# Fixed pads in front of the expert regions, a second silu for the rounded form, and router products placed among other products

## The reference

```python
x = x + 0.5 * moe(layernorm(x))      # first expert phase
x = x + attn(layernorm(x))           # attention block
x = x + 0.5 * moe(layernorm(x))      # second expert phase, the same weights

def moe(x):                          # 8 experts, hidden size 512, top 2
    logits = silu(x @ rw1 + rb1) @ rw2 + rb2
    w = softmax over the two largest logits, 0 elsewhere
    h = silu(x @ we1[e] + be1[e])
    return x + sum_e w[e] * (h @ we2[e] + be2[e])

def attn(x):                         # 16 heads of 64
    x = x + linear_attention(LN1(x)) # phi = elu + 1, causal: cumulative
                                     # sums of K V and K; num / den; @ Wo
    return x + gelu(LN2(x) @ Wf1) @ Wf2
```

## Time and profile before

| what | value |
|---|---|
| runs | 1998.72, 2001.55, 2002.62 us |
| profiled execution | 2005.34 us |
| its span | 2003.6 us |
| PE busy | 1698.4 us (85%) |
| DVE busy | 1558.9 us (78%) |
| ACT busy | 1072.6 us (54%) |
| POOL busy | 968.9 us (48%) |
| DMA, mean | 95 GB/s |

### The profile page before, as it was taken

How to read it: one execution, slowest core, us unless ns; L and a number is a source line. 1 busy time by engine, 2 the same in 40 slices (tenths; PEclk the granted TensorE clock), 3 DMA queues, 4 the chain that set the end, 5 groups by cost and what they waited for, 6 DMA issues and landing times. The chain is left out here.

```text
span 2003.6 us, 36381 instructions
## 1 busy us (share of the span) xinstructions
PE 1698.4 (85%) x12527; PEld 1384.7 (69%) x12527; DVE 1558.9 (78%) x4234; ACT 1072.6 (54%) x1935; POOL 968.9 (48%) x1010
## 2 busy tenths in 40 slices
PE   4448799984999999999999999999999956799990
PEld 3236688863778777777777777777777745687770
DVE  7667687765888888988888888898888626577774
ACT  2125577753556556555565555655556424577770
POOL 4876401115544465555546546445553324566661
PEclk9998899996999999999999999999999967899995
DMA  7554677740000010000001001001000004577757
GB/s 228 190 179 132 227 254 263 264 156 13 12 9 9 9 20 18 11 19 19 12 16 20 16 12 21 18 9 20 17 12 12 12 11 180 201 235 249 231 195 266
DMA packets 91664, 190.31 MB, mean 95 GB/s; under 512 B 15021, under 2 KB 52570, under 8 KB 80474
## 3 DMA queue, kind: packets, MB, share of 16 engines
q1 hardware_dynamic: 45738, 131.26, 19.3%
q0 software_dynamic: 33840, 46.17, 8.7%
q10 hardware_dynamic: 11904, 10.55, 1.5%
HBM read 131.08 MB, written 56.85 MB: 94 GB/s over the span
## 5 line engine op out<-in xcount | busy, mean ns | idle before, releaser
L1551 POOL TENSOR_TENSOR at_sc<-at_sc 128x512 f32<-128x512 f32 x128 | 198.2, 1548 | 344.4 <-DVE at_sc L1651 344.1
L551 ACT ACTIVATE f_hid<-f_up_ps,f_w 128x512 f32<-128x512 f32 x312 | 214.3, 688 | 155.0 <-PE f_up_ps L426 126.3
L1643 DVE SCALAR_TENSOR_TENSOR at_qk<-at_exps,at_relus 128x512 f32<-128x512 f32 x256 | 182.8, 715 | 100.5 <-ACT at_relus L1460 97.9
L1651 DVE TENSOR_TENSOR at_sc<-at_s_ps,mask 128x384 f32<-128x384 f32 x512 | 251.7, 550 | 1.1 <-PE at_s_ps L1284 1.1
L892 DVE TENSOR_TENSOR f_hid_lo<-f_hid,f_hid_hi 128x512 fp32r<-128x512 f32 x312 | 209.2, 688 | 14.8 <-ACT f_hid_hi L558 3.1
L665 POOL DMA_INDIRECT expert_rows<-f_rows_out,f_dest x156 | 165.3, 1059 | 97.1 <-DVE f_rows_out L915 60.5
L1958 POOL DMA_INDIRECT x<-finished_rows,slot x120 | 195.7, 1631 | 29.7 <-issue 29.7
L1524 ACT ACTIVATE raw<-at_num_ps 128x512 f32<-128x512 f32 x128 | 76.1, 595 | 241.2 <-PE at_num_ps L1321 220.6
L648 POOL DMA_INDIRECT sent_rows<-f_xn,slot x144 | 148.8, 1034 | 69.5 <-issue 40.8
L1281 PE MATMUL at_s_ps<-at_qk 64*128 64x256 f32 x1024 | 172.0, 413 | 6.7 <-issue 4.3
L1459 ACT ACTIVATE at_exps<-at_proj_ps 128x512 f32<-128x512 f32 x253 | 152.4, 603 | 36.2 <-PE at_proj_ps L1259 29.4
(11 more groups left out here) (324 smaller groups left out, 4802.8 us busy)
## 6 DMA issues: line engine op xcount, KB each, us to landing
f_w<-split_weights SPq DMA_DIRECT2D x78, 1028.0 KB
f_got<-sent_rows SPq DMA_DIRECT2D x78, 264.0 KB, 4.7
finished_rows<-f_rows_out POOLq DMA_DIRECT2D x39, 256.0 KB, 2.5
split_weights<-f_split SPq DMA_DIRECT2D x8, 1024.0 KB
sent_rows<-f_pads SPq DMA_DIRECT2D x16, 264.0 KB
x<-in_L_attn_x SPq DMA_DIRECT2D x16, 256.0 KB, 5.1
raw<-in_L_ffn_we SPq DMA_DIRECT2D x16, 256.0 KB
out_x<-x ACTq DMA_DIRECT2D x16, 256.0 KB, 4.4
```

Source lines behind the costliest of these rows:

```text
L551: A(hid[:, c, :], up_bank(n)[:, :], ACT.Silu, bias=w[:, i % RING_W, 4 * HID + c:4 * HID + c + 1].bitcast(FP32)).then_inc(s_silu, 1)
L1551: g.tensor_tensor(sc[:, n % RING_SC, :, 3, :], sc[:, n % RING_SC, :, 1, :], sc[:, n % RING_SC, :, 2, :], ALU.add).then_inc(s_sum, 1)
L1643: stt(full, exps[:, p % 2, :], 1.0, relus[:, p % 2, :], ALU.min, ALU.add).then_inc(s_phi, 1)
L1651: last = tt(flat(sc[:, (n // 2) % RING_SC, 2 * (n % 2) + half, 0:3, :]), s_ps[2 * (n % 2) + half][:, 0:3 * P], flat(mask[:, :, :]), ALU.mult)
```

## The change

It has four parts.

1. **Pads.** `region_starts` is now 512 + e·REGION: every region has 512 pad records in front, at a fixed place, and the tail region has moved with it. The last tile of an expert no longer starts at a multiple of 512 from the region's start but 512 rows ahead of the region's end, so it ends with the expert's last row; where an expert has fewer than 512 rows it begins in the pad. Rows that the tile before has computed already are computed again. So no pads are written behind the regions: `pad_end`, `s_ends` and f2's pad records on POOL are gone. The fills of the front pads are issued by ACT at f1's start, and the eight of the tail region on ACT's queue at the end of iteration t = 9, after DVE has changed the token numbers in the pad records. DVE works out the clipped starts in the table, in f1 the moves of places have three steps for each expert (24 in place of 16), and in f2 rows that a tile does a second time get a destination that nothing reads (`dest_twice`, and `row_of`, `unused`, `done_rows` made once).
2. **Silu.** The high part is a second silu from the same PSUM bank, rounded on output, right behind the first one. ACT's copy and DVE's cast are gone; `low` waits for one semaphore, `s_hi`, and so does `up`, since the bank is read twice.
3. **Order of the joint stage.** The four logit products of a token tile stand between the products of `down` and `up` of the tile's first expert part, the wait for `s_r1` stands ahead of that part; `router_hidden` of the next tile is ahead of the fourth expert part; ACT applies the router's silu at the end of the iteration before and the gate's tanh after the first expert part; DVE reads the places ahead of `route(t, 1)`, and makes `x_lo` ahead of `route(t, 2)`.
4. **Attention.** A logit product stands behind the denominators of unit 0 and of unit 1, and the counts behind those of unit 2; the bank isn't cleared by them (`start=False`).

The diff, cut to its core:

```diff
@@ fills and tables
             def fill(engine, r, i):
-            engine.dma_start(k.sent[bass.ds(r, TILE), :].rearrange("(p q) d -> p (q d)", q=TQ),
+            engine.dma_start(k.sent[r:r + TILE, :].rearrange("(p q) d -> p (q d)", q=TQ),
-            def pad_end(e):
-                fill(sp, sp.value_load(ends[0:1, e:e + 1], min_val=0, max_val=E * REGION - TILE), e)
...
-                if i == with_rows + 2:
-                    sp.wait_ge(s_pads, n_pads)
-                    sp.wait_ge(s_ends, 1)
-                    for e in range(E):
-                        pad_end(e)
             sp.wait_ge(s_table, 4)
...
-            sp.wait_ge(s_ended, 16 * (2 * E if loads else E))
+            if loads:
+                sp.wait_ge(s_ended, 16 * 2 * E)
             load_rows(EARLY)
...
+                if before:
+                    tt(passed_counts[:, :, :], passed[:, own, :], count_steps[:, :].unsqueeze(1).broadcast_to([P, n, E]),
+                       ALU.mult).then_inc(s_tab, 1)
...
+                    step(base + 8)
+                    v.tensor_reduce(tile_count[:, :], passed_counts[:, :, :], AXIS_X, ALU.add).then_inc(s_tab, 1)
+                    step(base + 9)
+                    stt(tile_row[:, own], tiles_before[:, own], -float(TILE), rest_rows[:, :], ALU.mult, ALU.add).then_inc(s_tab, 1)
+                    step(base + 11)
+                    stt(clipped[:, :], tile_count[:, :], counts[:, 0:1], tile_row[:, own], ALU.add, ALU.min).then_inc(s_tab, 1)
+                    step(base + 12)
+                    if out is not None:
+                        tt(done_rows[:, own], tile_row[:, own], clipped[:, :], ALU.subtract)
@@ ACT: fills of the start, and of the tail region
-                    fill(act, E * REGION + i * TILE, i)
+                    fill(act, i * REGION, i)
...
+                if loads and t == 1 + E:
+                    act.wait_ge(s_pads, 4)
+                    for n in range(E):
+                        fill(act, E * REGION + TILE + n * TILE, n)
@@ ACT: silu and high
             def high(n):
-                act.wait_ge(s_silu, n + 1)
                 if n >= HC:
                     act.wait_ge(s_down, n - HC + 1)
-                A(hid_hi[:, n % HC, :], hid[:, n % HC, :], ACT.Copy).then_inc(s_hi_odd if n % 2 else s_hi_even, 1)
+                A(hid_hi[:, c, :], up_bank(n)[:, :], ACT.Silu,
+                  bias=w[:, i % RING_W, 4 * HID + c:4 * HID + c + 1].bitcast(FP32)).then_inc(s_hi, 1)
...
                     silu(m // HC, m % HC)
-                if m < ALONE:
                     high(m)
-                elif m % 2 == 0 and m - 1 >= ALONE and m - 1 < HC * NTILES:
-                    high(m - 1)
@@ DVE
-                if m >= ALONE and m % 2 == 0 and m < HC * NTILES:
-                    high_even(m)
@@ PE: up and down with the logits between
                 mm(u[:, :], hi, eT_hi[:, b, :], start=True, stop=False)
+                if t is not None:
+                    logits(2)
                 mm(u[:, :], hi, eT_lo[:, b, :], start=False, stop=False)
+                if t is not None:
+                    logits(3).then_inc(s_logit, 1)
...
                 mm(o[:, :], hi, hid_hi[:, c, :], start=(c == 0), stop=False)
+                if t is not None:
+                    logits(0)
                 mm(o[:, :], hi, hid_lo[:, c, :], start=False, stop=False)
+                if t is not None:
+                    logits(1)
@@ DVE, f2: place_rows
+                    stt(dest_twice[:, :], row_of[:, :], done_rows[:, i:i + 1], unused[:, i, :], ALU.is_lt, ALU.mult)
+                    last = stt(dest_once[:, :], is_first[:, :], -float(TOKENS), row[:, :, TOKEN], ALU.mult, ALU.add)
+                elif step == 4:
+                    last = tt(dest[:, i % RING_DEST, :], dest_once[:, :], dest_twice[:, :], ALU.max)
@@ attention: denominators
                         last = mm(num_ps[32 * j:32 * j + 32, 0:BT], den_sel[:, u, :], sc[:, (UNITS * s + u) % RING_SC, j, 0:4:3, :],
                                  start=(u == 0), stop=(u == UNITS - 1))
+                    if u < BQ and r is not None:
+                        logits(u)
+                    if u == BQ and t is not None:
+                        count_places(t)
```

More of the change, by code:

```diff
@@ L63, in ffn_phase @@
     T = k.tiles
-    RING_OUT = 5 if out is None else 7
+    RING_OUT = 4 if out is None else 7
     assert 2 * TILE * begin - E * (TILE - 1) > (EARLY - 1) * TILE
@@ L483, in _ @@
                 else:
+                    pe.wait_ge(s_route, 7 * order(T - 1) + 1)
                     pe.wait_ge(s_pl, 3 * order(T - 2) + 1)
+                if t < T and i >= 0:
+                    expert_part(i, 0, t)
+                elif i >= 0:
+                    expert_part(i, 0)
+                elif t < T:
+                    for q in range(TQ):
+                        last = logits(q)
+                    last.then_inc(s_logit, 1)
                 if t > start and t in (begin, T):
@@ L774, in _ @@
                     dve.wait_ge(zeroed, k.n_zeroed)
-                v.tensor_copy(pads[:, :, :, TOKEN], k.spare[:, E:2 * E, :] if loads else k.spare[:, 0:E, :]).then_inc(s_pads, 1)
+                v.tensor_copy(pads[:, :, :, TOKEN], k.spare[:, 0:E, :]).then_inc(s_pads, 1)
                 if loads:
@@ L930, in expert_part @@
                         place_rows(i, 2)
-                        if PLACED == 4:
+                        if out is not None:
                             place_rows(i, 3)
                     if m == at + 2:
-                        place_rows(i, PLACED)
+                        for part in range(3 if out is None else 4, PLACED + 1):
+                            place_rows(i, part)
                 for i in range(NTILES):
```

190 lines of the change are left out of this document (98 added, 92 removed).

## The result

The changed kernel takes 2034.01 us in the median of four runs (2030.47 to 2035.20), the kernel before 2001.35 (1998.72 to 2002.62): ratio 1.0166, 95% interval 1.0148 to 1.0183. The changed kernel is slower by 33 us. The forecast was 1995, 6.5 us faster, with a range that ended at 2013.

The account below looks back on a forecast made before the run. PE was taken as the limit wherever nothing holds it up. Terms −11 − 5 + 1 + 16 − 5 − 3 = −7 took the profiled 2005.34 us to 1998.3, 1994.5 in the median, say 1995; range 1978 to 2013.

Parts of the forecast that it names:

- late row loads: Steady expert tiles, both phases: copy-out behind two silus on ACT delays SP's row loads; +16 us, bounds 0 and +36.
- Rival A: Steady expert tiles: row loads come the whole 0.58 us late, costing 36 us in place of 16; 2014.5 us, chance 0.15.
- central case: Whole kernel: all terms as estimated, about 1995 us, own range 1987 to 2003, chance 0.35.
- −3: Attention: logits' weight loads hidden beside denominators (at most −15) against array shape changes (+9); taken as −3 us.
- Rival B: Attention: changes of array shape drain TensorE, +9 us in place of a 3 us gain; 2006.5 us, chance 0.12.
- −11: Second phase's start: pads off SP's queue end PE's wait for rows; −11 us, bounds −16 and −7.
- Rival C: Idle stretches without releaser stay, only moved: second phase's pads −8, first phase's 0; 2002.5 us, chance 0.20.
- Pads in the first phase: End of first phase's routing: pad writes off SP recover part of 12.0 us lost; −5 us, bounds 0 and −10.
- the table's and the moves' extra steps: Longer table of tiles costs 1.2 us in each phase's pad term; DVE's extra moves of places cost nothing.
- the fills at +1: First phase's pure routing stage: eight pad writes on ACT's queue, mostly hidden; +1 us, bounds 0 and +5.
- The joint order's −5: Joint stage of routing and expert tiles: PE's wait for `f_places` shrinks; −5 us, bounds −14 and +5.

Follow-up runs that it names:

- second pair of traces: Changed kernel and kernel before, both unedited, run and traced again on one chip: 2038.03 us and 2011.42 us.
- second group: Follow-up runs on one chip where the kernel before took 2008.57 us; the unedited changed kernel took 2038.03 us there, ratio 1.0152.

## Why the prediction was wrong

**Silu twice: right mechanism, a second wait put at nothing.** The step was "late row loads", +16. Measured are +11.0 and +14.4 (+8.4 and +13.9 in the second pair of traces), 25 in all, and +18.7 for this part alone in a group without idle times. The forecast followed `s_outT` to SP's queue and did not ask who else waits for it. PE does, at the transposes back. In the first phase's stage 262 to 440 the wait for rows grew by 6.5 us (1.2 to 7.7), where the forecast had 6.4; the 5.7 for the copy-out, 17 times 0.33, came on top. (In the second phase both waits are there too, but the view puts a part of them down to "issue", so their shares are not read there.) So the term of the sum that failed is this one: slack of 0.29 at the transposes back against a copy-out later by 0.58. It could have been read from the kernel before, from the copy-out's end at 303.00 to the transposes back at 303.35; the view of waits could not show it, since nothing waited there yet. Rival A had the sign, and by row loads alone 36 us, 2014.5, with a chance of 0.15. Measured distances of tiles (6.89 and 7.08) lie between the central case's (6.7 and 6.9) and A's (7.0 and 7.2), so it had the size no better than the forecast, and not the mechanism.

**Attention: the sign was wrong.** −3 was taken "nearer to nothing than to either end"; it is +6.7 in the first comparison, +7.2 in the second group and +11.2 in the group without idle times. Rival B had +9 by 0.11 for each change of shape, and this is what happened: 0.12 for each, in steps with two to five changes more. That the stage with idle times shows only 7 of it has no cause shown. The hope that the logits' weight load hides beside wide denominators failed: a pair takes 0.32 among them and 0.27 ahead of them, and the denominators themselves go slower in pieces. The rule of the Trainium skill ("TensorEngine Tiling (Array Packing)", Key Properties) that a change of mode drains TensorE agrees with these traces, at 0.12 us a change. I had weighed it and set it below my own estimate, though the one row that I had pointed the same way.

**Pads, second phase: the wait went and another took its room.** −11 was 8.9 for the wait and its low clock, 3.7 as a share of ACT's idle time, less 1.2. The wait went from 6.93 to 1.33. But POOL's run of indirect DMAs had more to do, since the rows of two tiles were ready for it when the sendings ended, not of one: 24 issues without a break in 32 us, where the kernel before had 20 in 27, and ACT stood idle twice beside them. The step that failed is the room: the forecast took it that PE would go on as soon as no pads held the row load, and credited 0.6 of ACT's idle time to the pads as well. Rival C said that idle times without a releaser stay, and gave −8 for them; they stayed, and in this pair they grew (6.64 and 4.47 became 9.40 and 4.37; 5.86 and 4.50 became 12.20 in the second pair). That they grew because POOL's run did is argued, not shown. I had the evidence in the joint stage: `f_lg` on DVE starting 1.4 after POOL's last sending. I used it for that stage only. Without idle times there was no wait to win: the pads alone changed nothing (1.0012).

**What held.** Pads in the first phase, in sign: −5 forecast, −4.7 measured, but −13.7 in the second pair of traces, where the kernel before had lost more, so that −4.7 fits so well is luck. Then the table's and the moves' extra steps (nothing to be seen), the fills at +1 against +2.5 with the joint order in it. The joint order's −5 came to −0.7, within its bounds; its own condition, that POOL's sendings hold the iteration and earlier logits gain nothing, fits the traces: six joint tiles take 48 to 50 us in the groups without idle times and 61 to 65 in those with them, whichever order they have. The wait only changed its place. In the view of waits of 140 to 212 us, first before, then after:

```profile
DVE f_lg L718 <- remote: 16.3, 4, 5.2
```

```profile
DVE f_places L766 <- remote: 14.2, 4, 4.2
```

`f_lg` no longer waits, since the read of places ahead of it does, until 1.2 us after POOL's last sending (162.72 + 0.96 to 164.90).

**The sum.** −11, −5, −3 and −5 forecast became −1, −5, +7 and −1, and +16 became +25. By these stretches the change cost 29.6 where −7 was forecast. Attention and the pads of the second phase had their rivals with the right direction on paper, and the joint order its bounds; the copy-out at the transposes back had nothing.

**The better kernel.** The smallest edit of all, the copy-out one step earlier on the kernel before, beats both, the kernel before by little: 0.9946 in one group, 0.9983 in another. With the pads it is 0.9958, with pads, second silu and joint order but attention as before 0.9961. The intervals of the last two overlap those of the first, so the three kernels can't be ranked.

## What to carry to other kernels

When an instruction is put ahead of another in an engine's queue, list everyone that waits for the one behind it, not only the chain that was looked at first, and read the slack of each in the timeline, from the end of the one to the start of the other. A view of waits lists only those whose slack is already gone. Keep products of one array shape together: here each change of shape cost 0.12 us, and small products among the wide ones hid nothing. Where an engine is idle with its inputs ready, look at what the others do until it starts again before crediting that time to any edit.

## What was not expected of the hardware

ACT and DVE stand idle, ready, while POOL issues indirect DMAs without a break (1.27 us each, some longer). At the start of the second phase ACT's last idle stretch there ends 1.8 to 2.8 us after the last issue (1.2 to 1.4 for DVE in the joint stage of f1, in the two iterations read); earlier ones end in the midst of a run. This is in two of five groups and in the first comparison, in all eight traces of them, and absent from the other three groups. In the twelve traces of those three the run is longer still, 36 to 44 issues in 48 to 61 us, the tiles beside it are mostly 6.4 to 7.5 us apart from the sixth on, and neither ACT nor DVE has an idle stretch of over 1.5 us beside it that is put down to "remote". So the run does not do it alone. There `f_lg` starts in the midst of a run (154.57, between POOL's issues at 153.49 and 154.79, in the kernel with the pads alone):

```profile
153.49 1.00 POOL L662 DMA_INDIRECT sent_rows<-f_xn,slot  x1 [0.30 <-issue]
154.57 0.18 DVE L732 TENSOR_TENSOR f_lg<-f_up_ps,rb 128x32 f32<-128x32 f32 x1
154.79 0.96 POOL L662 DMA_INDIRECT sent_rows<-f_xn,slot  x1 [0.30 <-issue]
```

The kernel before differs by 55 to 63 us between such groups. Where this lies is seen from one kernel that was traced in both, the kernel before with the early copy-out (spans of 1937.3 and 2001.5):

| stretch | without | with idle times |
|---|---|---|
| start, f1 | 135.29 | 139.23 |
| six joint tiles of f1 | 48.47 | 60.95 |
| next four, end of routing | 34.84 | 48.20 |
| last 28 tiles of f1 | 182.84 | 181.38 |
| attention | 1074.55 | 1096.19 |
| first six tiles of f2 | 43.59 | 57.34 |
| last 32 tiles of f2 | 207.30 | 208.30 |

It is all in the stages in which POOL sends routed rows; the steady stages are as long in both. Who compares two kernels whose stages of this kind differ has to have both conditions, or he reads one effect for the other. What the two conditions are, and by what POOL's run holds the other engines, the runs don't tell: moving the run moved the stall, but no run took it away.
